# RWKV group norm: centring moved into the value weights, value products of own heads only, one variance per token and head

## The reference

```python
x = x + xattn(_layernorm(x), ctx)
x = x + rwkv(_layernorm(x))
x = x + ffn(_layernorm(x))

def rwkv(x):                      # H = 16 heads, N = 8 channels a head, Q = T = 64
    xx = shifted(x) - x
    r = (x + xx * maa_r) @ Wr.T;  k = (x + xx * maa_k) @ Wk.T
    v = (x + xx * maa_v) @ Wv.T;  g = gelu((x + xx * maa_g) @ Wg.T)
    att = r @ k                   # per head, 64 x 64
    y = att * Wmat @ v            # Wmat[h]: decay powers below the diagonal, u on it
    mean = y.mean(axis=-1); var = y.var(axis=-1)      # over a head's 8 channels
    yn = (y - mean) / sqrt(var + 64e-5) * ln_w + ln_b
    return (yn * g) @ Wo.T
```

## Time and profile before

| | |
|---|---|
| median of 3 runs | 466.17 us (465.69 to 466.52) |
| profiled execution: its time, its span | 466.76 us, 465.0 us |
| TensorE matmul busy | 321.6 us (69%), 3844 records |
| TensorE weight loads busy | 261.6 us (56%) |
| VectorE busy | 253.6 us (55%), 526 |
| ScalarE busy | 205.0 us (44%), 409 |
| GpSimd busy | 114.1 us (25%), 133 |

### The profile page before, as it was taken

One profiled execution on the slowest core, in us unless ns is written; L12 is line 12 of the kernel. 1 busy time (PEld: TensorE's weight loads), 2 busy tenths in 40 slices (PEclk: granted clock), 3 DMA queues, 4 the chain that ended last, 5 costly groups with the idle time before them and its releaser, 6 DMA issues.

```text
span 465.0 us, 9098 instructions
## 1 busy us (share of the span) xinstructions
PE 321.6 (69%) x3844; PEld 261.6 (56%) x3844; DVE 253.6 (55%) x526; ACT 205.0 (44%) x409; POOL 114.1 (25%) x133
## 2 busy tenths in 40 slices
PE   1775687776677778795868677696785757667554
PEld 1655667654665567574755476565664735554244
DVE  3353446628475746645664946566657473363541
ACT  2753424624374353724382455636555252332231
POOL 1155414402232213303141222312222122020000
PEclk9959799978898969986998879989998867776566
DMA  8600000000000000000000000000000000000000
GB/s 287 235 1 3 0 2 3 0 1 1 1 2 1 2 1 14 0 1 1 1 13 1 1 1 13 1 1 1 13 2 1 1 11 1 1 11 2 0 12 11
DMA packets 4072, 7.69 MB, mean 17 GB/s; under 512 B 704, under 2 KB 2368, under 8 KB 4032
## 3 DMA queue, kind: packets, MB, share of 16 engines
q1 hardware_dynamic: 3456, 5.53, 3.3%
q10 hardware_dynamic: 576, 1.59, 1.0%
HBM read 6.06 MB, written 1.05 MB: 15 GB/s over the span
## 4 chain that ended last, share of the span: by engine, by line
PE 42%; DVE 26%; ACT 20%; issue 7%; POOL 3%; DMA 1%; POOLq 0%; SPq 0%; DVEq 0%; ACTq 0%
PE bank L299 7%; PE bank L264 6%; DVE xn_tok L717 6%; DVE s_sb L756 4%; PE bank L334 4%; PE bank L402 4%; DVE yT L822 4%; ACT o_sb L555 3%; DVE sd L828 3%; ACT w_raw L570 3%; ACT q_sb L534 2%; DVE w_raw L806 2%; ACT e_sb L542 2%; PE bank L358 2%; PE bank L238 2%
## 5 line engine op out<-in xcount | busy, mean ns | idle before, releaser
L299 PE MATMUL bank<-wo_sb,o_sb 128*128 128x128 f32 x256 | 43.7, 341 | 25.1 <-ACT o_sb L555 25.1
L548 ACT ACTIVATE pT_sb<-bank 128x512 f32<-128x512 f32 x32 | 18.2, 597 | 96.3 <-PE bank L273 96.3
L299 PEld LDWEIGHTS bank<-wo_sb,o_sb 128*128 128x128 f32 x256 | 40.6, 249 | 32.5 <-ACT o_sb L555 32.5
L991 POOL TENSOR_TENSOR s_sb<-s_sb,s_max 128x1024 f32<-128x1024 f32 x16 | 30.6, 1915 | 102.4 <-DVE s_max L762 102.4
L748 DVE TENSOR_TENSOR v_sb<-bank,bv_bc 128x512 f32<-128x512 f32 x32 | 21.5, 686 | 39.5 <-PE bank L252 39.4
L982 POOL TENSOR_SCALAR ln_var<-ln_mv 128x2 f32<-128x2 f32 x32 | 6.1, 191 | 148.6 <-DVE ln_mv L712 147.7
L997 POOL TENSOR_TENSOR e_sb<-e_sb,s_rec 128x1024 f32<-128x1024 f32 x16 | 30.4, 1901 | 46.2 <-DVE s_rec L770 46.2
L264 PEld LDWEIGHTS bank<-k_sb,q_sb 64*64 64x64 f32 x1024 | 34.7, 145 | 9.1 <-issue 6.6
L264 PE MATMUL bank<-k_sb,q_sb 64*64 64x64 f32 x1024 | 37.9, 231 | 1.5 <-DVE s_sb L756 1.5
L238 PE MATMUL bank<-cT_lo,w_hi 128*128 128x256 f32 x64 | 23.4, 366 | 20.9 <-DVE w_lo L726 10.1
L534 ACT ACTIVATE k_sb<-bank,col 128x256 f32<-128x256 f32 x64 | 26.9, 479 | 24.1 <-PE bank L240 24.1
(11 more groups left out here) (109 smaller groups left out, 786.5 us busy)
## 6 DMA issues: line engine op xcount, KB each, us to landing
out_tok<-x_tok SPq DMA_DIRECT2D x8, 128.0 KB, 1.9
w_raw<-in_w_k ACTq DMA_DIRECT2D x1, 512.0 KB, 4.9
w_raw<-in_w_q ACTq DMA_DIRECT2D x1, 512.0 KB, 6.4
w_raw<-in_w_v ACTq DMA_DIRECT2D x1, 512.0 KB, 8.0
bv_bc<-in_rows SPq DMA_DIRECT2D x1, 512.0 KB, 8.5
x_tok<-in_x SPq DMA_DIRECT2D x1, 512.0 KB, 10.3
cT<-in_ctxT SPq DMA_DIRECT2D x1, 512.0 KB, 11.1
wo_sb<-in_w_o SPq DMA_DIRECT2D x1, 512.0 KB, 11.8
```

The lines of the kernel that those rows point to most:

```text
L299: mm = engine.matmul(b[:, 0:D], o_sb[:, t % 2, c, :], wo_sb[:, c, :], start=(c == 0), stop=(c == HP - 1))
L991: engine.tensor_tensor(s_sb[:, t % 2, :, :, :], s_sb[:, t % 2, :, :, :], s_max[:, t % 2, :, :].unsqueeze(3).to_broadcast([P, HP, 2, T]), A ...
```

## The change

- The value weights are multiplied once with `centre` before the stages (`centre_v`, copied by ACT to `wv_c`), so v has no mean within a head, and y has none either. `centring` per group goes.
- `kv` writes k as before and v into `v_own`: four copies with room between them, zeroed once by POOL, copy m holding the channels of heads m, m+4, m+8, m+12. `mix_values` does 64 products of 64 columns, accumulating over m, instead of 16 of 256, and the two banks hold y itself. `own_head` goes.
- ACT's `squares` reads both banks and writes `sq` and `yT`; `variance` makes one value per token and head (tokens on partitions, 16 columns a tile); ACT's `root` takes Ln and then Exp with scale -0.5, repeated for 8 channels; PE's `spread` transposes that back, and `group_norm` multiplies with it, from PSUM, without a reciprocal.
- `diag` and `ternary` now lie in `hT`; the eight banks are one tensor.

```diff
@@ constants and tiles
-    c[:, C_AVG:C_ONES] = same
+    c[:, C_AVG:C_AVG + RH] = (i[:, None] // RN == np.arange(RH)[None, :]).astype(np.float32) / RN
...
+        v_own = sb("v_own", [P, 2, GT, HG * (D + RN)])
+        wv_c = sb("wv_c", [P, D])
...
@@ tensor: rwkv_kv
-                pe.wait_ge(ld_wrk, 16)
+                pe.wait_ge(centred, 1)
...
@@ tensor: mix_values and what follows
                 for par in range(2):
-                    take(later_banks, ("mixval", g, par), own_ok, 8 * g + 4 * par + 4)
+                    take(later_banks, ("mixval", g, par), y_ok, g + 1)
+                for par in range(2):
+                    at["mixval", g, par] = later_banks.banks[par]
                 for half in range(2):
+                    for n in (2 * half, 2 * half + 1):
+                        pe.wait_ge(decayed, 4 * g + n + 1)
                     for tt in range(GT):
-                        for n in (2 * half, 2 * half + 1):
-                            pe.wait_ge(decayed, 4 * g + n + 1)
-                            for par in range(2):
-                                mm = engine.matmul(
-                                    bank[at["mixval", g, par]][32 * n:32 * n + 32, tt * HG * T:(tt + 1) * HG * T],
-                                    kv_sb[par * T:par * T + T, g % 2, 1, tt * D + 32 * n:tt * D + 32 * n + 32],
-                                    attw[par * T:par * T + T, n, tt, :], start=True, stop=True,
-                                    tile_position=(par * T, 32 * n))
+                        for m in range(HG):
+                            for n in (2 * half, 2 * half + 1):
+                                for par in range(2):
+                                    rows = slice(par * T, par * T + T)
+                                    mm = engine.matmul(
+                                        bank[at["mixval", g, par]][32 * n:32 * n + 32, tt * T:(tt + 1) * T],
+                                        v_own[rows, g % 2, tt, m * D + 32 * n:m * D + 32 * n + 32],
+                                        attw[rows, n, tt, m * T:(m + 1) * T], start=(m == 0), stop=(m == HG - 1),
+                                        tile_position=(par * T, 32 * n))
                 mm.then_inc(mixval_mm, 1)
...
-            def centring(g):
-                b = take(later_banks, ("centre", g), centred, g + 1)
-                pe.wait_ge(own_ok, 8 * g + 8)
-                engine.matmul(b[:, 0:GTOK], centre, yT[:, :], start=True, stop=True).then_inc(centre_mm, 1)
...
             def variance(g):
-                b = take(later_banks, ("var", g), root_ok, g + 1)
+                b = take(later_banks, ("var", g), logged, g + 1)
                 pe.wait_ge(squared, g + 1)
-                engine.matmul(b[:, 0:GTOK], average, sq[:, :], start=True, stop=True).then_inc(var_mm, 1)
+                for j in range(GT):
+                    mm = engine.matmul(b[:, j * RH:(j + 1) * RH], sq[:, j * P:(j + 1) * P], average, start=True,
+                                       stop=True)
+                mm.then_inc(var_mm, 1)
...
+            def spread(g):
+                b = take(later_banks, ("spread", g), gn_scaled, g + 1)
+                pe.wait_ge(root_ok, g + 1)
+                for j in range(GT):
+                    mm = engine.transpose(b[:, j * P:(j + 1) * P],
+                                          gn_rstd[:, j * RH:(j + 1) * RH, :].rearrange("p h c -> p (h c)"), ident)
+                mm.then_inc(spread_mm, 1)
+
+            def centre_v():
+                b = take(later_banks, "centre", centred, 1)
+                pe.wait_ge(ld_const, 16)
+                pe.wait_ge(ld_wrk, 16)
+                engine.matmul(b[:, 0:D], wrk[:, 2, :], centre, start=True, stop=True).then_inc(centre_mm, 1)
...
             mean_abs(1)
+            centre_v()
             turn_x(1)
...
@@ scalar
+            def squares(g):
+                act.wait_ge(mixval_mm, g + 1)
                 act.wait_ge(var_mm, g)
...
+                engine.activation(batches(sq[:, :]), y, ACT.Square).then_inc(squared, 1)
+                act.wait_ge(gn_scaled, g)
+                engine.activation(batches(yT[:, :]), y, ACT.Copy).then_inc(y_ok, 1)
...
-                engine.activation(sd[:, :], bank[at["var", g]][:, 0:GTOK], ACT.Sqrt,
-                                  bias=const[:, C_GNEPS:C_GNEPS + 1]).then_inc(root_ok, 1)
+                flat_var = bank[at["var", g]][:, 0:GT * RH]
+                engine.activation(gn_log[:, :], flat_var, ACT.Ln,
+                                  bias=const[:, C_GNEPS:C_GNEPS + 1]).then_inc(logged, 1)
+                act.wait_ge(logged, g + 1)
+                act.wait_ge(spread_mm, g)
+                engine.activation(gn_rstd[:, :, :], gn_log[:, :].unsqueeze(2).to_broadcast([P, GT * RH, RN]), ACT.Exp,
+                                  scale=-0.5).then_inc(root_ok, 1)
...
@@ vector: kv, group_norm
+                engine.tensor_copy(kT_sb[:, g % 2, :], b[:, 0:GTOK])
+                for j in range(GT):
+                    own = v_own[:, g % 2, j, :].rearrange("p (m q) -> p m q", m=HG)[:, :, 0:D]
+                    op = engine.tensor_copy(own.rearrange("p m (n k) -> p m n k", n=NGR)[:, :, :, 0:RN],
+                                            b[:, GTOK + j * D:GTOK + (j + 1) * D].rearrange(
+                                                "p (n m c) -> p m n c", n=NGR, m=HG))
+                op.then_inc(kv_ok, 1)
...
-                engine.reciprocal(sd[:, :], sd[:, :]).then_inc(gn_inv, 1)
...
+                engine.scalar_tensor_tensor(out=z1[:, :], in0=yT[:, :], scalar=col[:, COL_GNW:COL_GNW + 1],
+                                            in1=bank[at["spread", g]][:, 0:GTOK], op0=ALU.mult,
+                                            op1=ALU.mult).then_inc(gn_scaled, 1)
...
@@ gpsimd, first instructions
             engine.memset(xs[:, :, :, 0:1], 0.0).then_inc(zero_ok, 1)
+            engine.memset(v_own[:, :, :, :], 0.0).then_inc(zero_ok, 1)
```

More of the change, by code:

```diff
@@ L150, in build_block @@
         minus_half = sb("minus_half", [P, GT])
-        bank = [stack.enter_context(nc.psum_tensor(f"bank{i}", [P, 512], F32)) for i in range(8)]
+        psum = stack.enter_context(nc.psum_tensor("bank", [P, 8, 512], F32))
+        bank = [psum[:, i, :] for i in range(8)]
         ident = const[:, C_ID:C_ID + P]
         centre = const[:, C_CEN:C_CEN + P]
-        average = const[:, C_AVG:C_AVG + P]
+        average = const[:, C_AVG:C_AVG + RH]
+        batches = lambda v: v.rearrange("p (t b i) -> p b t i", b=2, t=GT)
         flat = lambda v: v.rearrange("p t d -> p (t d)")
@@ L314, in rwkv_kv @@
                     mm = engine.matmul(b[:, GTOK + j * D:GTOK + (j + 1) * D], mixed[:, 1, j * P:(j + 1) * P],
-                                       wrk[:, 2, :], start=True, stop=True)
+                                       wv_c[:, :], start=True, stop=True)
                 mm.then_inc(kv_mm, 1)
@@ L493, in tensor @@
                 if rwkv:
-                    centring(s - 1)
+                    variance(s - 1)
                 if now:
@@ L497, in tensor @@
                 if rwkv:
-                    variance(s - 1)
+                    spread(s - 1)
                 if ffn:
@@ L644, in scalar @@
             mean_abs(1, wpr_raw[:, :], ld_proj)
+            act.wait_ge(centre_mm, 1)
+            engine.activation(wv_c[:, :], bank[at["centre"]][:, 0:D], ACT.Copy).then_inc(centred, 1)
             split_c(1)
@@ L689, in scalar @@
                 if rwkv:
-                    spread(s - 1)
+                    squares(s - 1)
                 if now:
@@ L797, in kv @@
                 dve.wait_ge(mixval_mm, g - 1)
-                engine.tensor_copy(kv_sb[:, g % 2, :, :],
-                                   bank[at["kv", g]][:, :].rearrange("p (a n) -> p a n", a=2)).then_inc(kv_ok, 1)
+                dve.wait_ge(zero_ok, 2)
+                b = bank[at["kv", g]]
+                engine.tensor_copy(kT_sb[:, g % 2, :], b[:, 0:GTOK])
[5 more added lines that the diff above has]
+                op.then_inc(kv_ok, 1)
             def decay(g, n):
@@ L835, in group_norm @@
                 dve.wait_ge(rwkv_mm, g)
-                engine.scalar_tensor_tensor(out=zT[:, :], in0=yc[:, :], scalar=col[:, COL_GNB:COL_GNB + 1],
+                engine.scalar_tensor_tensor(out=zT[:, :], in0=z1[:, :], scalar=col[:, COL_GNB:COL_GNB + 1],
                                             in1=g_sb[:, g % 2, :], op0=ALU.add, op1=ALU.mult).then_inc(gated, 1)
@@ L946, in vector @@
                     apply_x(s + 3)
-                if rwkv:
-                    own_head(s - 1, 0)
-                    own_head(s - 1, 1)
                 if ffn:
@@ L1125 @@
         "cols": cols,
-        "w_rwkv": lines(np.concatenate([n("attn_W" + m).T for m in "rkvgo"], axis=1)),
+        "w_rwkv": lines(np.concatenate([n("attn_W" + m).T if m != "v" else n("attn_Wv") for m in "rkvgo"], axis=1)),
```

50 lines of the change are left out of this document (15 added, 35 removed).

## The result

The changed kernel takes **433.4 us** (median of 4 runs, 427.1 to 434.5) against 466.4 (465.7 to 468.3): 0.922 of the time before, 95% interval 0.910 to 0.933. Forecast were 427.0, with a range of 417 to 440. The ratios leave out executions more than 1.5% slower than the fastest of the same kernel, and so aren't quite the quotients of the medians. The first profiled execution has a span of 432.0 us, that of r_after 423.2, with the same instructions; where these 8.8 us come from is the second half of what follows.

A forecast was written before the change was run, and what follows sets the result against it. No engine is full; a relay among PE, DVE and ACT bounds the kernel. Tails 31.2 plus middle 7.8 make 39.0 off the profiled 466.76, 427.8, so 427 us at the median; range 417 to 440.

The forecast's parts named there:

- Squares earlier, 3.2 a stage: Tail: without own heads and centring, `sq` starts right behind `exponent`, 3.2 us earlier in stages 1 to 4.
- `mix_values` at 18 ns a record, 2.3 us: 128 records of 64 columns take 2.3 us, 1.2 more than now, hidden in stages 1 to 6.
- C: Rival, chance 0.12: `mix_values` takes 32 ns a record, or Ln and Exp are dearer; 433 us.
- E: Rival, chance 0.05: accumulating `mix_values` products run one behind the other, 16.1 us a group; slower, 529 us.
- `o_sb` to `rwkv_out`, 8.25 to 5.85: Tail: variance ahead, Ln, Exp, spread and a full-clock output product save 2.4 us each in stages 1 to 4.
- A: Rival, chance 0.15: the clock stays low during the output product, 0.5 to 1.0 more in four stages; 430 us.
- The middle, 7.8: Stages 2 to 7: the table load ahead of the middle's exponent goes, 1.3 us in each of six.
- B: Rival, chance 0.10: the middle gives nothing, as DVE's sum of exponents and mixes are late there; 435 us.
- Hidden edits: `kv` copies 0.3 us more, POOL's memset 4.1 in idle time, `centre_v` 0 to 0.5 at the start; all counted as nothing.
- rival D: Chance 0.05: every table switch drains the engine first, 1.28 us each; 440 us.

The follow-up runs named there:

- r_after: The changed kernel itself, unedited, run again beside other kernels on one chip: 429.2 us, 0.913 of before.
- a1_centre: The kernel before with only the centring moved into the value weights; own heads on DVE and old norm stay: 456.7 us, 0.973.
- a2_order: a1_centre with one more line moved, the variance product ahead of the output product on PE: 437.8 us, 0.934.
- u1_norm: The changed kernel with the old norm back (full-width variance, Sqrt, reciprocal on DVE, no spread): 426.5 us, 0.909.
- u2_one_set: The changed kernel with own heads back on DVE and one table set for Exp and Ln: 423.5 us, 0.900.
- t_one_set: The changed kernel with a hand-written load of the table set holding both Exp and Ln ahead of the tail's exponent: 412.0 us, 0.877.
- u2_own: The changed kernel with 16 products over all heads and eight own-head operations on DVE back: 432.6 us, 0.919.

## Why the prediction was near, and where its steps were wrong

**The sum by stages.** The forecast span was 465.0 - 39.0 = 426.0; the profiled one is 432.0, that of r_after 423.2. Start to first scores: forecast 37.4, measured 36.2 and 35.9. Stage 0: 39.6; 43.0 and 39.6. Stages 1 to 4: 175.6; 177.5 and 175.9. Stage 5: 44.3; 44.9 and 44.9. Stage 6: 40.5; 41.8 and 40.9. Stage 7 to the end: 88.7; 88.6 and 86.1. The 6 us are 3.4 in stage 0 and 3.9 in stages 1 to 6, less 1.2 at the start. Stage 0 of the kernel before, of the changed one and of r_after:

```profile
37.40:77.02 39.62, 25.82 (x432) 22.77 (x431) 19.68 (x36) 14.01 (x29) 16.31 (x14) 0.91 0.01 1
```

```profile
36.24:79.22 42.98, 29.19 (x432) 25.54 (x431) 20.11 (x38) 14.13 (x30) 18.38 (x17) 0.85 0.01 1
```

```profile
35.85:75.46 39.61, 25.85 (x432) 22.79 (x431) 19.68 (x36) 14.13 (x30) 18.42 (x16) 0.91 0.01 1
```

The 432 matmul records are the same, and they are busy 3.3 us longer at clock 0.85. So the distance of median and forecast is within what one kernel's executions differ by, in where the low clock falls. No term of the sum had this in it; the range held the result, but was worked out from other things, and that 427 came so near is in part luck.

The forecast for a full stage was 44.3; r_after has 44.5, 44.2 and 44.6 in stages 3, 2 and 4. Stage 3 of the first profile, at clock 1.00, has 42.6. The difference lies mostly between `attend` and `exponent`, 16.8 from the start of the one to the end of the other in the kernel before and in r_after (195.44 to 212.20, 180.21 to 196.98), and 15.25 in that stage (184.53 to 199.78): both kernels have a low stretch there (clock 0.50 from 199 to 202 before, 0.54 from 183.5 to 186.5 in r_after). The forecast took it over from the kernel before without pricing it.

**Squares earlier, 3.2 a stage:** held; `sq` starts with the end of `e_sb`. But what it is worth isn't additive. It is made of the centring (a1_centre, 12 us, where 11.4 were expected) and the own heads (a2_order to u1_norm, 11 us; u2_one_set to t_one_set, 11; u2_own to the changed kernel, 0 to 3). In u2_own the two loads cover the cold output product, and the low clock lies under them and not elsewhere; in the others it isn't so. The tail alone shows the parts more evenly. From the end of `e_sb` to `rwkv_out`, stage 3:

| kernel | us | change, by |
|---|---|---|
| before | 13.08 | |
| a1_centre | 11.48 | -1.60, centring |
| a2_order | 8.71 | -2.77, order |
| u1_norm | 6.27 | -2.44, own heads |
| changed, both profiles | 7.11 | +0.84, new norm with two loads |
| t_one_set | 5.68 | -1.43, without the two loads |

So the forecast's 5.6 for this stretch (3.2 and 2.4) is 5.97 measured.

**`mix_values` at 18 ns a record, 2.3 us:** it is 15 ns and 1.9, and hidden; C and E fall. In stage 8, at the low clock, it takes 3.24.

**`o_sb` to `rwkv_out`, 8.25 to 5.85:** measured 5.6, and the output product warm, so A falls as it was put (it takes 2.02 in stages 1, 3, 4 and 5, 2.54 in stage 2 and 3.76 in stage 6 of the first profile). The clock does stay low in other places, which A didn't have. The number is right; what it was worked out from misses the cause. The prediction named the variance's new place in half a sentence and costed Ln, Exp and spread at length; the experiments give the place 19 us, and the new norm, loads of the middle included, nothing that can be told. The missing line of working was the same chain with the old norm: load 1.28, Sqrt 0.47, reciprocal 1.75, scaling and gate 1.0, which is 4.5, shorter than the 5.0 to the gate of the new one.

**The middle, 7.8:** held in the main; `e_sb` follows `x_hi` without a load, and B falls, since what `attend` waits for is still the gate. By the start of `attend`, counted from the first scores, stages 2 to 7 gain 7.4 in all in r_after, but only 4.4 in the first profile, where the low clock took more of it. It is what pays for the second load of the tail.

**Hidden edits:** held. The `kv` copies are 0.42 and 2 of 0.24, the memset 1.91 in POOL's first idle time, and the centring of the weights costs nothing that the rows show.

**Drain, rival D:** no. Where the engine works up to a load, Ln starts 0.01 behind it (201.32 + 1.28, 202.61). The Trainium skill (ScalarE: Activation LUTs, What ACT_TABLE_LOAD costs) has about 1.38 us of drain for each switch; no row here shows it. The Trainium skill's rule on the same page (Table sets: the hidden batching unit), that ln followed by exp needs a single load, is right as a statement on the sets. t_one_set shows what the common set is worth: both loads behind `o_sb` gone in each tail, 17 us with the clock's part, where the prediction had 10 for one load. Here it held only once the load was written out by hand.

## What to carry to other kernels

Before costing a new formula, work out the old one in the new order: a product that stands behind a longer one on an in-order engine can be the whole wait, and here moving it gave 19 of some 38 us. What an edit saves depends on what else is as long beside it and on where the low clock goes, so undo parts from both ends; the same product for own heads was worth 0 to 3 us with the two loads in the tail and 11 without. Short idle times of TensorE can cost twice, by themselves and by the clock afterwards (429.2 us against 416.8 with some of them filled); look at the granted clock of equal stages before taking a few us for the effect of an edit.
